# A fused transformer kernel on one core: the causal stage's preparation of batch 0 is moved into the last steps of the cross attention before it

## The reference, cut to what matters

```python
x = x + cross_attention(layernorm(x), ctx)        # 16 heads of 16, keys from ctx
# causal block
nx = layernorm(layernorm(x)) * ln1_w + ln1_b      # two norms in a row, folded into one scale and shift
q, k, v = split(nx @ Wqkv + bqkv)
scores = where(causal, q @ k.T / 4, min)
x2 = layernorm(x)
x2 = x2 + softmax(scores) @ v @ Wo + bo
nx2 = layernorm(x2) * ln2_w + ln2_b
x = x + x2 + moe(nx2)                             # top 2 of 8 experts
x = x + cross_attention(layernorm(x), ctx)        # 8 heads of 64
x = x + fp6_linear(x)
```

## Time and profile before

| | us |
|---|---|
| median of 3 runs (lowest to highest) | 1969.74 (1966.71 to 1970.39) |
| the profiled execution | 1969.25 |
| its span, first to last instruction | 1967.4 |
| TensorE busy | 1872.3 |
| DVE busy | 1495.6 |
| ScalarE busy | 1270.8 |
| GpSimd busy | 953.1 |
| mean granted TensorE clock | 0.977 |

### The profile page before, as it was taken

The page is one execution under the profiler, slowest core; times in us unless marked ns, Lnnn a source line. Parts: engine busy times, 40 slices in busy tenths (PEclk is TensorE's granted clock), DMA queues, the critical chain, the costliest instruction groups (busy, mean ns, idle before and its releaser), DMA issues.

```text
span 1967.4 us, 61539 instructions
## 1 busy us (share of the span) xinstructions
PE 1872.3 (95%) x20887; PEld 1642.5 (83%) x20887; DVE 1495.6 (76%) x3438; ACT 1270.8 (65%) x2720; POOL 953.1 (48%) x1616
## 2 busy tenths in 40 slices
PE   7999999999699999879999999969999999999996
PEld 5888888888578788679999999958888888888885
DVE  6778878887278887756766666657888888888886
ACT  2555555555377777657777777747777777777773
POOL 4566556655246766640000000057766767676751
PEclk9999999999799999889999999979999999999998
DMA  8222332231050111165565555421111111111100
GB/s 236 90 88 87 109 95 87 87 111 40 1 182 28 37 40 36 61 237 190 187 202 197 188 205 194 160 82 55 36 41 34 40 34 30 42 32 40 34 15 10
DMA packets 116596, 182.05 MB, mean 93 GB/s; under 512 B 10851, under 2 KB 94563, under 8 KB 116067
## 3 DMA queue, kind: packets, MB, share of 16 engines
q1 hardware_dynamic: 110386, 166.51, 26.6%
q0 software_dynamic: 6144, 14.69, 2.5%
HBM read 127.68 MB, written 53.48 MB: 92 GB/s over the span
## 4 chain that ended last, share of the span: by engine, by line
PE 52%; DVE 2%; issue 1%; ACT 1%; POOL 1%; DMA 0%; DVEq 0%; ACTq 0%; POOLq 0%; SPq 0%
PE ps_quad L1423 11%; PE ps_out L1443 9%; PE ps_quad L182 6%; PE ps_quad L102 4%; PE ps_out L114 4%; PE ps_turned L108 4%; PE ps_quad L1874 3%; PE ps_turned L182 3%; PE ps_proj L1894 3%; PE ps_proj L182 2%; PE ps_proj L1899 1%; DVE c_negmax L119 1%; PE ps_proj L1431 1%; ACT c_probs L134 0%; DVE e_w2L L1369 0%
## 5 line engine op out<-in xcount | busy, mean ns | idle before, releaser
L1423 PE MATMUL ps_quad<-e_xT,w 128*128 128x128 f32 x2016 | 235.3, 275 | 1.7 <-DVE e_xT L1381 1.7
L1423 PEld LDWEIGHTS ps_quad<-e_xT,w 128*128 128x128 f32 x2016 | 230.4, 192 | 2.2 <-DVE e_xT L1381 2.2
L364 ACT ACTIVATE a_probsT<-ps_quad 125x1792 f32<-125x1792 f32 x96 | 159.9, 1666 | 100.6 <-PE ps_quad L533 100.6
L1563 POOL TENSOR_TENSOR c_held<-minus_half 1x1 f32<-1x1 f32 x32 | 9.4, 294 | 410.8 <-DMA slots<-e_y 408.3
L1338 ACT ACTIVATE e_act_T<-ps_quad,fc_b 128x128 f32<-128x128 f32 x504 | 137.3, 384 | 94.2 <-PE ps_quad L1423 94.2
L134 ACT ACTIVATE c_probs<-ps_quad,c_negmax 112x375 f32<-112x375 f32 x256 | 143.8, 572 | 64.6 <-DVE c_negmax L119 64.6
L1443 PE MATMUL ps_out<-e_w2H,e_aH 128*128 128x256 f32 x504 | 149.1, 296 | 8.9 <-DVE e_w2L L1369 8.9
L126 DVE TENSOR_SCALAR c_probs<-c_probs,c_recip 112x375 f32<-112x375 f32 x256 | 151.5, 632 | 4.5
L1369 DVE TENSOR_TENSOR e_w2L<-w,e_w2H 128x1024 fp32r<-128x1024 f32 x126 | 151.4, 1243 | 0.0
L421 DVE TENSOR_REDUCE a_negmax<-ps_turned 112x2 f32<-112x750 f32 x128 | 120.1, 938 | 34.2 <-PE ps_turned L519 34.0
L119 DVE TENSOR_REDUCE c_negmax<-ps_quad 112x2 f32<-112x750 f32 x128 | 113.9, 930 | 40.0 <-PE ps_quad L102 39.5
(11 more groups left out here) (350 smaller groups left out, 6025.1 us busy)
## 6 DMA issues: line engine op xcount, KB each, us to landing
w<-in_fc_t SPq DMA_DIRECT2D x71, 1024.0 KB, 4.9
slots<-a_zeros SPq DMA_DIRECT2D x60, 512.0 KB, 4.9
a_cT<-in_ctx_t SPq DMA_DIRECT2D x32, 375.0 KB, 3.5
c_cT<-in_ctx_t SPq DMA_DIRECT2D x32, 375.0 KB, 3.2
e_xg<-slots SPq DMA_DIRECT2D x63, 128.0 KB, 3.9
slots<-e_y SPq DMA_DIRECT2D x63, 128.0 KB, 1.8
out<-c_fo SPq DMA_DIRECT2D x32, 112.0 KB, 1.9
residual<-in_x SPq DMA_DIRECT2D x1, 2912.0 KB, 20.7
```

The source lines that it names most:

```text
L364: act.activation(probsT[:, 2 * i:2 * i + 2, :, :].rearrange("p c r x -> p r c x"), quad[0:KC, :, 0:2 * HALF].rearrange("p r (c x) -> p r c ...
L1423: last = pe.matmul(hidden[par][:, c // 4, (c % 4) * TILE:(c % 4 + 1) * TILE], mem["w1"][:, par, k, c * 128:(c + 1) * 128], xT[par][:, k, : ...
```

## The change

The first stage gets hooks at fixed places of its last steps, and the causal stage hands it functions through `mem`. All of what the steps -2 and -1 and the set-up did is now called from there, and the second stage starts with step 0.

- ScalarE: at the start of step 30 the copy of `choice` and `nn` of batch 0; at the start of step 31 `nT`; after the exp of step 31 `q`, `kT`, `q_high`; after the copy of `oT` the `nn` of batch 1.
- TensorE, all in step 31: at its start the transposes of `nn` of batch 0 and the bias product; after the scores the q and k products; after the value products the mask into `quad`; after the transposes to rows the V product and the transposes of `nn` of batch 1.
- DVE: constants, the copy of `bv_t` and the sum of the bias at the start of step 31. Its step 32 (moments of batch 31) is no longer run in the first stage but within the causal stage's step 0, after the maxima.
- GpSimd: masked `qT` and `k_high` of batch 0 at the start of step 32, ahead of the residual add of batch 31. `double_norm(31)` is called in the causal stage's step 0, after the masked tiles of batch 1.
- The bias product goes to `bias_ps = pc[0:T, 0:D]` and not to `outs`, and so doesn't wait for the first stage's last output; the first value product of the causal stage does that now.
- SP's load of the first expert weights waits also for all `rates_ready` and `slots_cleared`.

The core of the diff (hooks in the first stage first):

```diff
 # cross_first, gpsimd step
+                    if isinstance(b, int) and b == NB:
+                        mem["causal_gpsimd"](pool)
                     if exists(b - 1):
                         pool.wait_ge(o_biased, b)
...
-                    if exists(b - 1):
+                    if exists(b - 1) and not (isinstance(b, int) and b == NB):
                         double_norm(b - 1)
+                mem["last_rates"] = lambda: double_norm(NB - 1)
 # cross_first, scalar step
+                    if isinstance(b, int) and b == NB - 2:
+                        mem["causal_scalar"](act, 0)
+                    if isinstance(b, int) and b == NB - 1:
+                        mem["causal_scalar"](act, 1)
                     if exists(b):
                         exp(b, 2)
+                    if isinstance(b, int) and b == NB - 1:
+                        mem["causal_scalar"](act, 2)
...
+                    if isinstance(b, int) and b == NB - 1:
+                        mem["causal_scalar"](act, 3)
                     if exists(b):
                         act.wait_ge(oT2_mm, b + 1)
 # cross_first, vector
+                    if isinstance(b, int) and b == NB - 1:
+                        mem["causal_vector"](dve)
...
-                over_batches(dve, step, 3, 1, 4, 4)
+                over_batches(dve, step, 3, 0, 4, 4)
+                mem["last_moments"] = lambda: step(NB, 0)
 # cross_first, tensor step: causal_tensor(pe, 0) before scores(par, 2), (pe, 1) after it,
 # (pe, 2) after values(par, 1), (pe, 3) after the transposes to rows, all for b == NB - 1
 # self_attention
+        bias_ps = pc[0:T, 0:D]
+        def first_tensor(pe, part):
+            if part == 0:
+                pe.wait_ge(weights_in, 16 * len(loads))
+                pe.wait_ge(wo_in, 16)
+                pe.wait_ge(mem["first_v"], 2 * NB)
+                pe.wait_ge(mem["first_q"], NB)
+                rows_turn(pe, 0)
+                pe.wait_ge(mem["first_shift"], 2 * NB)
+                pe.wait_ge(mem["first_max"], 6 * NB)
+                pe.wait_ge(mem["first_xT"], NB)
+                pe.wait_ge(cleared, 2)
+                pe.wait_ge(bias_step, 1)
+                for k in range(2):
+                    last = pe.matmul(bias_ps, oT2[:, k, :], wo[:, k, :], start=(k == 0), stop=(k == 1))
+                last.then_inc(bias_mm, 1)
+            if part == 1:
+                pe.wait_ge(nT_ready, 1)
+                qk_product(pe, pb, 0, q_mm)
+                qk_product(pe, pa, 2, k_mm)
+            if part == 2:
+                pe.wait_ge(mem["first_exp"], 3 * NB)
+                plain_mask(pe)
+            if part == 3:
+                pe.wait_ge(q_rounded, 1)
+                for k in range(2):
+                    last = pe.matmul(pb[0:T, 0:D], nT[:, k, :], wqkv[:, k, 2 * D:3 * D], start=(k == 0), stop=(k == 1))
+                last.then_inc(v_mm, 1)
+                pe.wait_ge(k_ready, 1)
+                rows_turn(pe, 1)
+        def first_scalar(act, part):
+            if part == 0:
+                act.wait_ge(weights_in, 16 * len(loads))
+                act.activation(choice[:, :, :], choice_raw, ACT.Copy).then_inc(cleared, 1)
+                rows_scaled(act, 0)
+            if part == 1:
+                act.wait_ge(nT_mm, 1)
...
+            if part == 2:
...
+            if part == 3:
+                rows_scaled(act, 1)
+        def first_gpsimd(pool):
+            pool.memset(zero[:, :], 0.0).then_inc(consts, 1)
+            pool.wait_ge(consts, 1)
+            pool.wait_ge(cleared, 1)
+            masked_queries(pool, 0, 0)                         # lines 789 to 797 for batch 0
 # self_attention, sync
                 sp.wait_ge(values_mm, 1)
+                sp.wait_ge(rates_ready, NB)
+                sp.wait_ge(mem["slots_cleared"], 32 * (NB - 2))
 # self_attention, the engines' steps
+                    if isinstance(b, int) and b == 0:
+                        mem["last_rates"]()                    # gpsimd, after masked_queries(pool, nxt, 1 - par)
...
+                    if isinstance(b, int) and b == 0:
+                        mem["last_moments"]()                  # vector, after the maxima
...
+                        if isinstance(b, int) and b == 1:
+                            pe.wait_ge(mem["first_done"], NB)  # tensor, before values(1 - par)
...
-                over_batches(pool, step, 2, 4, 4)              # and the same for scalar, vector, tensor
+                over_batches(pool, step, 0, 4, 4)
```

More of the change, by code:

```diff
@@ L731, in self_attention, with rows_turn, qk_product @@
         ]
+        def rows_turn(pe, n):
+            pe.wait_ge(nn_ready, n + 1)
+            for k in range(2):
+                last = pe.transpose(pa[:, k * T:(k + 1) * T], nn[:, k * 128:(k + 1) * 128], ident[0:T, 0:T])
+            last.then_inc(nT_mm, 1)
+        def qk_product(pe, dst, first, done):
+            for t in range(2):
+                for k in range(2):
+                    at = (first + t) * 128
+                    last = pe.matmul(dst[:, t * T:(t + 1) * T], wqkv[:, k, at:at + 128], nT[:, k, :],
+                                     start=(k == 0), stop=(k == 1))
+            last.then_inc(done, 1)
@@ new lines, in rows_scaled @@
+        def rows_scaled(act, n):
+            act.wait_ge(rates_ready, n + 1)
+            wait(act, nT_mm, n)
+            act.activation(nn[:, :], row(residual, n), ACT.Identity,
+                           scale=row(rates, n)[:, 1:2], bias=row(shifts, n)[:, 1:2]).then_inc(nn_ready, 1)
+        def first_scalar(act, part):
[5 more added lines that the diff above has]
+                act.wait_ge(nT_mm, 1)
+                for k in range(2):
+                    last = act.activation(nT[:, k, :], pa[:, k * T:(k + 1) * T], ACT.Identity,
+                                          scale=ln1w[:, k:k + 1], bias=ln1b[:, k:k + 1])
+                last.then_inc(nT_ready, 1)
+            if part == 2:
+                act.wait_ge(q_mm, 1)
+                for t in range(2):
+                    last = act.activation(q[:, t, :], pb[:, t * T:(t + 1) * T], ACT.Identity, bias=bqk[:, t:t + 1])
+                last.then_inc(q_whole, 1)
+                act.wait_ge(k_mm, 1)
+                for t in range(2):
+                    last = act.activation(kT[0][:, t, :], pa[:, t * T:(t + 1) * T], ACT.Identity,
+                                          bias=bqk[:, 2 + t:3 + t])
+                last.then_inc(k_ready, 1)
+                for t in range(2):
+                    last = act.activation(q_high[:, t, :], pb[:, t * T:(t + 1) * T], ACT.Identity, bias=bqk[:, t:t + 1])
+                last.then_inc(q_rounded, 1)
+            if part == 3:
+                rows_scaled(act, 1)
@@ new lines, in first_vector @@
+        def first_vector(dve):
+            for i in range(2):
+                dve.memset(v[i][:, :, HD:HD + 1], 1.0)
+                dve.memset(v[i][:, :, HD + 1:32], 0.0)
+            dve.memset(ones[:, :], 1.0)
+            dve.memset(mem["ones"][:, :], 1.0)
+            dve.memset(negmax[:, :], 0.0)
+            dve.memset(earlier[:, :], 0.0).then_inc(cleared, 1)
+            dve.wait_ge(cleared, 2)
+            dve.wait_ge(weights_in, 16 * len(loads))
+            dve.tensor_copy(oT2[:, :, :], bv_t[:, :].unsqueeze(2).to_broadcast([128, 2, T])).then_inc(bias_step, 1)
+            dve.wait_ge(bias_mm, 1)
+            dve.tensor_tensor(bo[0:T, :], bo[0:T, :], bias_ps, ALU.add).then_inc(bias_step, 1)
+            dve.wait_ge(bias_step, 2)
@@ L860, in step @@
                     if exists(ahead):
-                        act.wait_ge(rates_ready, ahead + 1)
-                        wait(act, nT_mm, ahead)
-                        act.activation(nn[:, :], row(residual, ahead), ACT.Identity,
-                                       scale=row(rates, ahead)[:, 1:2], bias=row(shifts, ahead)[:, 1:2]).then_inc(nn_ready, 1)
+                        rows_scaled(act, ahead)
                     if exists(nxt):
@@ L1044, in _ @@
             def _(pe):
-                pe.wait_ge(weights_in, 16 * len(loads))
-                pe.wait_ge(cleared, 2)
-                pe.wait_ge(wo_in, 16)
-                pe.wait_ge(mem["first_done"], NB)
-                pe.wait_ge(bias_step, 1)
-                for k in range(2):
-                    last = pe.matmul(outs[0:T, D:2 * D], oT2[:, k, :], wo[:, k, :], start=(k == 0), stop=(k == 1))
-                last.then_inc(bias_mm, 1)
                 pe.wait_ge(bias_step, 2)
```

84 lines of the change are left out of this document (36 added, 48 removed).

## The result

The changed kernel takes 1955.03 us (median of 4 runs, 1952.96 to 1957.26), the kernel before 1968.64 us over the runs made beside it (4 runs, 1966.71 to 1970.39). The ratio is 0.9931, with a 95% interval of 0.9919 to 0.9943: 13.6 us faster, and by the interval between 11 and 16 us. Repeated on another chip it was 1957.27 against 1968.70, again a ratio of 0.9931 (0.9914 to 0.9948).

The account below looks back on a forecast made before the run. The prediction took the hand-over to be bound by a relay of engines working one at a time, at half clock. 15.65 us saved less 1.9 for the clock gave 13.7, hence 1956.0 us on the median's scale; range 1951.5 to 1962.5.

Parts of the forecast that it names:

- ScalarE's work in step 30: Copy of choice and nn of batch 0, 1.2 us, fit ScalarE's 1.24 us idle before the exp: cost 0.
- DVE's set-up: Memsets and copy for the bias product in step 31, done by 503.7, before TensorE needs them at 504.35: cost 0.
- GpSimd came last: At the causal stage's start, masks behind batch 30's rates end at 518.5; plain scores of batch 0 at about 518.6.
- The clock fell: A fall to half clock between 515 and 518.6, as the causal stage starts, costing 1.9 us; bounds 0 and about 4.
- Shifted by one constant: Sign in the new profile: the rest of the trace after the hand-over moves by one constant.
- full-clock sum: First plain scores of the causal stage at 518.6 instead of 534.25, TensorE at full clock: 15.65 us saved.
- A relay at half clock is cheap, full work at half clock is not.: Premise for pricing the clock at the hand-over, where one engine works at a time; no size of its own.
- Rival D: Causal stage starts cold and stays cold, 7.5 us more per batch at half clock; slower, 1976.6 us; chance 0.03.
- these 19.1 us: Stretch from the last first-stage product (515.17) to the first plain scores (534.25), which the change attacks.
- A (clock never lost): No clock cost at the causal stage's start: 15.65 us saved, 1954.1 us on the median's scale; chance 0.16.
- B (half clock throughout): TensorE at half clock from 505 on: gain 9.1 us, 1960.6 us on the median's scale; chance 0.21.
- C: Masks wait behind later rates, or second stage's first steps idle anyway: under 3.9 us left, 1967 us; chance 0.08.

Follow-up runs that it names:

- fill: The changed kernel with 20 identity transposes on TensorE in its 2.3 us wait for GpSimd's masked k; 1952.46 us, ratio 0.9908.
- before_warm: The kernel before with nothing moved, but 44 extra identity transposes in TensorE's idle times of the hand-over; 1961.47 us, ratio 0.9964.
- prep_late: The changed kernel with the preparation of batch 0 again behind the first stage, set-up, bias product, nn and its transposes still early; 1955.01 us, ratio 0.9928.
- masks_first: The changed kernel with GpSimd's masked q and k of batch 0 in step 31, ahead of the rates of batch 30; 1949.72 us, ratio 0.9900.
- prep_late_2: prep_late run again unchanged, to see whether it holds the clock; no time given, clock 0.90 from 495 to 530 us.
- masks_first_hold: masks_first with 8 and 5 identity transposes added in two idle times of TensorE in step 30; 1950.26 us, ratio 0.9904.
- hold_2: masks_first_hold run again unchanged; 1950.56 us, ratio 0.9910.

## Why the prediction was right, point by point

It said 1956.0 us, and 1955.03 was measured; 15.65 us less at the first plain scores, and 15.70 were measured; 13.7 at the second, measured 13.65. In part this is luck between terms, and in part luck with the execution: in the second trace of the changed kernel the same two numbers are 14.40 and 12.67 us.

**Held.** ScalarE's work in step 30 cost nothing. DVE's set-up was ready in time. GpSimd came last, with the masks at 0.89 and 0.93 and 0.1 for the memset: from the end of the rates (517.87) to the plain scores 2.08 us, predicted 2.1. The clock fell between 519 and 520, when the causal stage started, and cost 2.06 us (fill) where 1.9 were set. The old periods came back. They are about 9.13 us in the mean; the 9.03 of the prediction is the first of them only, and in both traces the one behind it is 9.58. "Shifted by one constant" holds for the later stages only to some 4 us, the scatter told above.

**Sizes off, and cancelling.** I had no fall before 515. There was one, earlier than the one of the old trace: in step 30, seen in its output product (2.03 and 2.05 us in the two traces of the changed kernel) and in the window from 503 to 505.5. It came and went in executions of one kernel and delayed the bias product by 0.7 us in the first trace and 2.1 in the second. It was made up in the first by rows that I had summed by their printed lengths: q and k products took 1.97 us and not 2.24 (508.93 to 510.90), values 2.43 and not 2.72 (to 513.33), and V, transposes and mask overlap likewise. So the full-clock sum was met with the clock at half for a part of it. An estimate from the places of the bias product: with the clock held in step 30, as it was in the old trace, the first plain scores would come 0.7 us earlier, and the gain there would be 16.4 us and not 15.65.

**Wrong: "A relay at half clock is cheap, full work at half clock is not."** This step had no effect on the sum, since the sum went from endpoint to endpoint, but it told the story wrongly. Filling the old idle times alone gave 5.1 us in the trace and 7 in the time (before_warm), because in a relay the products are on the path too. Rival D built on the same sentence, and misread the rows: the old half clock didn't end in the pre-steps. It was still 0.50 at 535 and reached into the first k product of step 0,

```profile
534.90 1.45 PE L1100 MATMUL ps_turned<-s_nT,s_wqkv 128*128 128x112 f32 x8
```

so the old kernel paid a part of that price as well (its difference is 8.52 and not 8.19 us). D's "8.9 us slower than the full-clock sum" should also be 22.5, by its own 15.65 - 22.5 = -6.9.

I had also called what was removed "these 19.1 us", as if its parts added. They don't: from the start of the output product to the plain scores it is 19.08 us in the old trace; with the clock held 14.35 (before_warm); with the set-up, `nn` and its transposes forward as well 6.03 (prep_late); with the preparation forward too and the masks first 1.02 (masks_first). The changed kernel has 3.39, as it waits 2.3 us for GpSimd. So, taken in this order, the clock is worth 4.7 us, the move of the set-up with `nn` and its transposes 8.3 (no run parts them), and the move of the preparation 5.0, less the 1.3 us by which it delays the output product. Of these 3.7 us the changed kernel kept 1.35 at the first plain scores, the rest went into the wait for GpSimd, and at the second plain scores the fall that followed took it all.

**The rivals.** A (clock never lost) is what the changed kernel would be with the gap filled and no fall in step 30; it was seen in no trace of that kernel. B (half clock throughout) did not happen, nor C and D. But the gap that decided between them, GpSimd's 2.3 us, was one reordered call away from being gone: masks_first has the lowest times of all, with a ratio of 0.9900 and again 0.9907 to the kernel before, 5 to 6 us under the changed kernel.

## What to carry to other kernels

At a hand-over between stages look first for engines working one at a time, and price that chain at the TensorE clock that the idle times bring with them: filling them with useless products is a cheap test of how much of a stall is clock. Parts of such a chain cover each other, so undo them one at a time before saying which one paid; and after moving work look for the new last arrival in its queue, because what stands ahead of it there (here the rates, 1.66 us) may wait for something that it doesn't need.

## What the runs showed of the hardware

TensorE's granted clock was at its half level of 1.2 GHz or its full 2.4 GHz, and which of them a hand-over got changed between executions of the same kernel (prep_late 1.00, prep_late_2 0.90 over the same 35 us), with up to 2.1 us on the path. It fell behind idle times of TensorE, but not always at once and not behind all of them. In the old trace it fell between 504.5 and 505, some 0.9 us after TensorE had stopped. In the changed kernel's it fell between 519 and 519.5, some 1.8 us after TensorE had stopped, and between 502 and 502.5 with TensorE at full work since 501, behind 2 us with 0.6 us of work. In prep_late it stayed full from 495 to 530 us, with idle times of up to 1.2 us. With 20 transposes in the gap of 2.3 us (fill), or 13 in two gaps of step 30 (masks_first_hold, hold_2), it stayed up there in all three traces; of the twelve traces without the 13, two kept it in step 30 as well. "TensorE: Matmul & The Clock Gate", section "What's actually happening", in the Trainium skill says that activity releases the throttle, and these runs agree: in the changed kernel's trace it came back between 505.5 and 506, behind 2.50 us of work in the 2.50 us before.
